# Scattering edge records into cells: indirect DMAs written out one by one, with index and payload read where they lie

## The reference

```
deg = segment_sum(ones, dst)
h = relu(layernorm(x)); x = x + layernorm(h @ Wself.T + (segment_sum(h[src], dst) / deg) @ Wneigh.T + b)
h = relu(layernorm(x)); x = x + normalize(gcn(relu(gcn(h, W1, w)), W2, w))       # edge weight w
h = relu(layernorm(x)); x = x + batchnorm(gru(segment_sum(mlp([h[src], edge_attr]), dst), h))
h = relu(layernorm(x)); x = x + segment_sum(h[src] * w1, dst) @ W3.T + b3        # edge weight w1
```

## Time and profile before

| what | value |
| --- | --- |
| timed runs, median of 3 | 1393.64 us (1392.36 to 1397.23) |
| span of the profiled execution | 1375.1 us |
| median above the span | 18.5 us |
| PE busy | 1233.3 us (90%) |
| DVE busy | 1016.7 us (74%) |
| POOL busy | 704.1 us (51%) |
| ACT busy | 579.8 us (42%) |

### The profile page before, as it was taken

One profiled execution on the slowest core, in us unless ns is written; L12 is line 12 of the kernel. 1 busy time (PEld: TensorE's weight loads), 2 busy tenths in 40 slices (PEclk: granted clock), 3 DMA queues, 4 the chain that ended last, 5 costly groups with the idle time before them and its releaser, 6 DMA issues.

```text
span 1375.1 us, 20029 instructions
## 1 busy us (share of the span) xinstructions
PE 1233.3 (90%) x4504; PEld 751.2 (55%) x4504; DVE 1016.7 (74%) x1944; ACT 579.8 (42%) x1470; POOL 704.1 (51%) x827
## 2 busy tenths in 40 slices
PE   4867989338989889999999989999999899998998
PEld 2533444113333334456876745555555588886787
DVE  9698355138989989853358689999999899888543
ACT  0211221036666660122001168888888833334211
POOL 0577777767877771676677456666666200000000
PEclk9998999769999999999999999999999999999999
DMA  8851521130000006434222677777777300002231
GB/s 331 314 193 64 179 74 63 55 112 18 25 17 19 17 8 267 134 113 144 88 82 90 220 227 230 239 235 236 238 228 242 78 0 1 0 1 88 77 96 37
DMA packets 87257, 167.93 MB, mean 122 GB/s; under 512 B 16124, under 2 KB 44670, under 8 KB 84644
## 3 DMA queue, kind: packets, MB, share of 16 engines
q1 hardware_dynamic: 59588, 102.72, 22.2%
q0 software_dynamic: 25472, 59.97, 14.0%
q10 hardware_dynamic: 2144, 4.59, 1.2%
HBM read 115.97 MB, written 51.25 MB: 122 GB/s over the span
## 4 chain that ended last, share of the span: by engine, by line
PE 56%; issue 14%; POOL 10%; DVE 10%; DMA 5%; DVEq 2%; POOLq 1%; ACT 1%; SPq 0%; ACTq 0%
PE pb L1324 10%; POOL cell_rows L707 9%; PE pb L1224 6%; PE pb L1216 6%; PE pb L1419 5%; PE pb L1392 4%; PE pb L1393 4%; PE pb L1394 4%; PE pb L1338 3%; DVE arena L1675 3%; DMA cell_rows<-tiles,gidx 2%; PE pb L1340 2%; PE pb L1341 2%; PE pb L1190 2%; PE pb L1108 2%
## 5 line engine op out<-in xcount | busy, mean ns | idle before, releaser
L753 POOL DMA_INDIRECT dst_rows<-ering,gidx x168 | 169.4, 1008 | 103.1 <-issue 73.9
L707 POOL DMA_INDIRECT cell_rows<-tiles,gidx x168 | 169.3, 1008 | 68.0 <-issue 40.3
L1324 PE MATMUL pb<-arena 128*128 128x512 f32 x368 | 190.8, 602 | 2.3 <-ACT arena L975 2.3
L1675 DVE TENSOR_TENSOR arena<-pb,arena 128x384 f32 x272 | 151.8, 558 | 25.7 <-PE pb L1190 23.4
L1190 PE MATMUL pb<-arena 128*128 128x384 f32 x272 | 104.9, 512 | 43.8 <-POOL arena L760 43.8
L861 ACT ACTIVATE arena<-iota,free 128x128 f32<-128x128 f32 x272 | 94.3, 393 | 110.2 <-PE pb L1190 68.8
L806 POOL DMA_INDIRECT arena<-p_rows,arena x96 | 98.9, 1030 | 68.8 <-issue 26.7
L1816 DVE TENSOR_TENSOR arena<-pb,arena 128x512 f32<-128x512 f32 x184 | 122.0, 682 | 7.6 <-DMA arena<-p_rows,arena 5.3
L1190 PE MATMUL pb<-tiles,arena 128*128 128x384 f32 x272 | 102.4, 504 | 20.1 <-DVE arena L1675 18.3
L806 POOL DMA_INDIRECT arena<-p_rows,ws x88 | 91.4, 1038 | 44.5 <-issue 24.1
L1340 PE MATMUL pb<-high,low 128*128 128x512 f32 x138 | 108.0, 783 | 2.2 <-DVE arena L1831 1.7
(11 more groups left out here) (306 smaller groups left out, 2583.3 us busy)
## 6 DMA issues: line engine op xcount, KB each, us to landing
dst_rows<-arena SPq DMA_DIRECT2D x6, 2046.0 KB, 17.5
ering<-in_edge_attr_dram SPq DMA_DIRECT2D x41, 256.0 KB, 3.0
arena<-adj SPq DMA_DIRECT2D x10, 640.0 KB, 4.0
arena<-dst_rows SPq DMA_DIRECT2D x24, 264.0 KB, 4.2
arena<-wt_gru SPq DMA_DIRECT2D x48, 128.0 KB, 3.9
ws<-dst_rows SPq DMA_DIRECT2D x22, 264.0 KB, 4.2
arena<-in_x_dram SPq DMA_DIRECT2D x18, 256.0 KB, 9.3
arena<-in_L_gnn_W_hh_dram SPq DMA_DIRECT2D x3, 1024.0 KB, 20.0
```

What stands on the lines that cost most here:

```text
L707: nc.gpsimd.indirect_dma_start(cell_rows[:, :], bass.IndirectOffsetOnAxis(gidx[:, SPAN * a + k:SPAN * a + k + 1], 0), cring[:, a, k], None ...
L753: nc.gpsimd.indirect_dma_start(dst_rows[:, :], bass.IndirectOffsetOnAxis(gidx[:, k:k + 1], 0), ering[:, k, :], None).then_inc(e_scattered[ ...
L1324: nc.tensor.matmul(e_bank(k)[:], erowT[:, k % 4], w1e_sb, start=True, stop=True).then_inc(edge_mm, 1)
L1675: vtt(cell, pb[k % 4][:, 0:3 * P].rearrange("p (m d) -> p m d", m=3), cell, ALU.add).then_inc(block_added, 1)
```

## The change

The indirect DMA of column j now takes its index column straight from `idx1[:, j]` and its payload straight from `pay1[:, j]`. The copies, the payload ring, the semaphore `cells_indexed` and the loops are gone; the 168 DMAs stand in the program one after the other. All DMAs of the even spans raise `c_scattered[0]`, those of the odd spans `c_scattered[1]`, and a span waits at its start until all earlier spans of its parity have landed, so until the span before last has. SP waits for these two semaphores.

```diff
-        gidx = sb("gidx", [P, 2 * SPAN], I32)
-        cring = tiles[:, 3, 0:2 * SPAN * 4].rearrange("p (a c w) -> p a c w", a=2, c=SPAN)
+        gidx = sb("gidx", [P, COL], I32)
...
-        c_scattered = [[sem(f"c_scattered{a}_{k}") for k in range(SPAN)] for a in range(2)]
-        cells_indexed, edges_indexed = sem("cells_indexed"), sem("edges_indexed")
+        c_scattered = [sem(f"c_scattered{a}") for a in range(2)]
+        edges_indexed = sem("edges_indexed")
...
-            for a in range(2):
-                for k in range(SPAN):
-                    full = a == 0 or k < J - SPAN * (SPANS - 1)
-                    sp.wait_ge(c_scattered[a][k], 16 * (SPANS // 2 - (not full)))
+            sp.wait_ge(c_scattered[0], 16 * SPAN * (SPANS // 2))
+            sp.wait_ge(c_scattered[1], 16 * (J - SPAN * (SPANS // 2)))
...
-            def index_span(i, a, n=SPAN):
-
-                for k in range(n):
-                    at_least(pool, c_scattered[a][k], 16 * i)
-                passed()
-                c = bass.ds(SPAN * (2 * i + a), n)
-                nc.gpsimd.tensor_copy(cring[:, a, 0:n], pay1[:, c, :])
-                nc.gpsimd.tensor_copy(gidx[:, SPAN * a:SPAN * a + n], idx1[:, c]).then_inc(cells_indexed, 1)
-
-            def scatter_span(i, a, prepare_next, n=SPAN):
-
-                pool.wait_ge(cells_indexed, 2 * i + a + 1)
-                passed()
-                for k in range(n):
-                    nc.gpsimd.indirect_dma_start(cell_rows[:, :], bass.IndirectOffsetOnAxis(gidx[:, SPAN * a + k:SPAN * a + k + 1], 0),
-                                                 cring[:, a, k], None).then_inc(c_scattered[a][k], 16)
-                if prepare_next:
-                    prepare_next()
-
-            rest = J - SPAN * (SPANS - 1)
+            def scatter_span(span):
+
+                at_least(pool, c_scattered[span % 2], 16 * SPAN * (span // 2))
+                for j in range(SPAN * span, min(SPAN * span + SPAN, J)):
+                    nc.gpsimd.indirect_dma_start(cell_rows[:, :], bass.IndirectOffsetOnAxis(idx1[:, j:j + 1], 0),
+                                                 pay1[:, j], None).then_inc(c_scattered[span % 2], 16)
+
             for n in range(len(BATCHES) - 1):
-                first, last = BATCHES[n] // 2, BATCHES[n + 1] // 2 - 1
-                final = n == len(BATCHES) - 2
                 pool.wait_ge(order_ready[0], n + 1)
                 passed()
-                index_span(first, 0)
-                if last > first:
-                    with pool.Fori(first, last) as i:
-                        scatter_span(i, 0, lambda: index_span(i, 1))
-                        scatter_span(i, 1, lambda: index_span(i + 1, 0))
-                scatter_span(last, 0, lambda: index_span(last, 1, rest if final else SPAN))
-                scatter_span(last, 1, None, rest if final else SPAN)
-
+                for span in range(BATCHES[n], BATCHES[n + 1]):
+                    scatter_span(span)
```

## The result

The changed kernel took 1518.76 us (1517.38 to 1529.47, 4 runs) beside 1395.43 us for the kernel before (1392.36 to 1397.98, 4 runs): a ratio of 1.0909, 95% interval 1.0876 to 1.0942. It is **slower by 123 us**, where 26.5 us less were forecast.

The account below looks back on a forecast made before the run. POOL's own pace in the scatter was taken as the bound, about 33 us behind the next engine. Terms 27.1 + 0.6 - 0.8 - 0.8 = 26.1, or 26.9 from the whole stretch; 26.5 taken: 1393.64 - 26.5 = 1367.1 us, range 1363.5 to 1373.5.

Parts of the forecast that it names:

- Copies, their wait, the loops: POOL's scatter: at 33 boundaries between spans the step falls from 1.12 to 0.30 us, a gain of 27.1 us.
- The first DMA: Start of POOL's scatter: the first indirect DMA starts at about 42.4 instead of 42.99, 0.6 us won.
- The second batch: POOL's eleventh scatter DMA waits for DVE's second batch of indices and starts at 56.1: 0.8 us lost.
- Landings: Scatter: slow landings of a span's last DMA delay POOL at the span after next, 0.8 us lost in all.
- rival B: Scatter: the wait for landings binds in earnest, leaving gains of 8 to 22 us, 1372 to 1386 us; chance 0.09.
- DVE stays ahead from there on: Scatter: DVE's third index batch is complete at 68.3, 13 us after the second, while POOL needs 25 us for the second.
- so nothing new binds: End of the scatter: the table's load lands at 268.6 and DVE is ready at 262.17, 6.4 us before.
- It shifts as a whole: Behind the scatter: all that follows hangs on the table's load by semaphores, so the profiled span falls by 26.5 us.
- With the 18.5 us around it: Whole kernel: 18.5 us lie around the profiled span, so a span of 1348.6 us means a time of 1367.1 us.
- Rival A: The scatter's gain comes as worked out, 22 to 29 us, giving 1365 to 1372 us; chance 0.82.
- Rival C: Scatter: fetching written-out code stalls POOL, 8.0 us a stall; gain 10 to 19 us, or slower at four; chance 0.04.
- Rival D: Behind the table's load, something not tied to it takes 23 us or more; chance 0.03 of same, 0.02 of loss.

Follow-up runs that it names:

- x4_unrolled: The kernel before with only its loops written out, its copies, rings and ten semaphores kept: 1.0008 of the kernel before on chip 14.
- y2_half: The changed kernel with a memset of 430 columns on POOL ahead of each span: 0.9877 of the kernel before on chip 8.
- x1 to x3: The changed kernel with, in turn, a lone instruction after each wait, ten landing semaphores, a tiny memset between spans: 1.0882, 1.0862, 1.0867 of the kernel before, chip 14.
- x3: The changed kernel with a tiny memset on POOL between spans, which nobody waits for: 1.0867 of the kernel before on chip 14.
- y4: The changed kernel with a memset of 230 columns on POOL ahead of each indirect DMA: 1.0011 of the kernel before on chip 8.

## Why the prediction was wrong, point by point

The run on chip 8 (span 1344.2 us) shows the prediction's steps without PE's delay. The profile of before shown in front, span 1375.1, belongs with chips 8 and 4 by its marks: no "remote" wait, ranks done at 98.4 us, and a span like those there (1372 to 1382 us), although the times beside it, 1392 to 1397 us, are like those on 14 and 2. Which chip either pair ran on is not in its records.

Views of the run on chip 8: POOL's timeline, the chain (start, us, what), and the row of windows behind the load:

```profile
42.76 1.19 POOL L694 DMA_INDIRECT cell_rows<-pay,idx  x1 [39.48 <-DVE idx L1505]
...
55.72 0.97 POOL L694 DMA_INDIRECT cell_rows<-pay,idx  x1 [0.30 <-issue]
```

```profile
260.32 2.10 DMA cell_rows<-pay,idx
...
262.49 3.23 DMA free<-cell_rows
...
268.50 6.61 PE pb L1166 x14
```

```profile
262.00:280.00 18.00, 11.50 (x30) 6.47 (x30) 11.49 (x34) 11.00 (x31) 11.59 (x13) 0.72 0.60 213
```

- **Copies, their wait, the loops: right, 27.1 us.** The step is 0.30 at every boundary. From the first DMA's start to the last's it is 260.32 - 42.76 = 217.6 us, before 289.35 - 42.99 = 246.4: 28.8 us less, 27.1 of the copies and 1.7 less busy time in the DMAs (167.6 against 169.3). So **index and payload in place** cost nothing.
- **The first DMA: mis-sized.** The indices were done at 41.67 + 0.17 = 41.84 and the DMA started 0.92 us later, as the gather's did; but they were 0.35 us later than in the trace of before, so 0.2 us were won, not 0.6.
- **The second batch: mis-sized.** No wait at 55.72, where 0.8 us were to be lost: the indices came at 53.3 + 0.18 us instead of 55.2.
- **Landings: mis-sized, 0 in place of 0.8 us**, and rival B falls: neither here nor in the measured run do POOL's waits name a landing. The last DMA landed in 2.10 us. The Trainium skill (DMA: Bandwidth & Descriptors, section on the anatomy of one DMA on the GpSimd path) gives the fixed cost of a DMA as about 2.0 us; the trace agrees.
- **The load** starts at 262.49 (forecast 265), 29.2 us earlier than before. DVE waits 2.8 us for it (forecast 6.4; it was ready at 263.0), PE idles 14.0 us (17), and the rest of the program takes 1344.2 - 262.5 = 1081.7 us (1083.4). PE's clock in 262 to 280 us is 0.72, not 0.50, since PE starts within the stretch. The gain of 30.9 us in span is 4.4 above the sum. The ratio 0.9808 is 26.5 us of 1379.2, but its interval goes from 20 to 33 us, so that it meets the sum to the tenth is luck.
- **"DVE stays ahead from there on" and "so nothing new binds": the steps that failed**, on chips 14 and 2 and in the measurement itself. I took the pace of the engines that feed POOL from the trace of before, and it isn't theirs alone: DVE's batches hang on PE's ranks, and these came late while POOL's DMAs went on without a pause: after one wait of 26.0 us DVE's third batch, due at 68.3, came at 95.2, and later there was one span's ranks in 19.6 us. **"It shifts as a whole"** failed as well: the load of the table was no longer held by POOL's last landing but by PE's products ahead of it in SP's queue. The margin that I counted, 33 us of DVE and 44 us of PE, was the margin of an undisturbed PE. PE's products for the last store ended at 411.50 in place of 253.68, 158 us late, which used it up.
- **"With the 18.5 us around it": a misreading.** The time of each execution in these runs is 1.7 to 1.9 us above its own span. The 18.5 us were mostly the difference between two kinds of chip. The stretch behind the load shows it for the kernel before: 1395.5 - 291.2 = 1104.3 us on chip 14 (x4_unrolled), 1375.1 - 291.7 = 1083.4 in the profile in front; the changed kernel has 1516.6 - 413.8 = 1102.8. The 20 us lie where POOL issues the indirect DMAs of the gather. In the first 500 us behind the load PE is busy for 461.2 us in both kinds; in the next 300 us it executes 900 products in x4_unrolled and 948 in the profile of before (951 on chip 8, 907 in the measured run):

```profile
791.20:1091.20 300.00, 283.08 (x900) 146.10 (x899) 258.59 (x405) 235.13 (x711) 187.31 (x181) 0.99 0.72 220
791.70:1091.70 300.00, 291.74 (x948) 155.14 (x947) 272.79 (x426) 253.99 (x743) 190.27 (x184) 0.99 0.74 224
```

No "remote" wait is named in that stage, and no run tests what slows PE there. That the profile shown and the median shown differed by 1.3% was the one sign, in what I had, that the trace might not be of the machine that would be measured.
- **Rival A** is what the changed kernel shows on chip 8 and nowhere else. **Rival C** falls by x4_unrolled; the instruction queues fetched 27 and 25 pieces in the measured run, before 27 and 26, and none in the 60 us shown above. **Rival D** came nearest: a loss by something that the sum leaves out. But it looked behind the load, and the mechanism lay ahead of it. Its chance of a loss, 0.02, was too small for a stretch whose feeding engines had only been read in one undisturbed trace.

**Shown**: on chips 14 and 2 the loss comes from PE's late semaphores and starts during POOL's chains; on chip 14 the fused wait, the number of semaphores and the lack of a short instruction between spans are not its cause, nor is written-out code; on chip 8 neither the changed kernel nor any of its variants has the delay, and on chip 4 neither of the two variants run there. **Argued only**: that the unbroken pace is what the changed kernel adds. The phases begin 12 to 30 us into each chain and end near its end, and x4_unrolled, the kernel before with its loops written out, has them weakly on chip 14; but index and payload in place are as new as the pace, and no run separates the two on such a chip. **Open**: what in the chip holds PE's signals back, whether its recorder has a part in it (every timed execution was recorded, so none shows the kernel without it), and whether a longer pause prevents it. The versions with the pause of y2_half took 1.0 to 1.4% less than the kernel before on chips 8 and 4 and are untried on 14 and 2; a kernel that must run on all of them can't be chosen from these runs, and the kernel before is the only one known to lose nowhere.

## What to carry to other kernels

Before counting on an engine's slack, ask what feeds the engine that is being made faster, and whether that supply was measured under the new load; POOL's gain of 27 us was real and was worth minus 123 us where its suppliers fell behind. Put the changed kernel itself into every group of experiments as a control, and compare what the kernel before takes there: without it four good runs on another chip read like a cure. A span should fit the times beside it (in all runs here it is 1.7 to 1.9 us below its own time); where it doesn't, the profile is one of other circumstances.

## What was not expected of the hardware

- In the measured run, on chip 2 and on chip 14 (variants x1 to x3), a chain of indirect DMAs on POOL with gaps of 0.30 us (one in 1.27 us) goes with PE's instructions starting in steps of 0.70 us or multiples of it, and with its semaphores being seen late, in the measured run by 4.0 us at first and 16.6 us in the end. DVE's signals to PE arrive within 0.1 us at the same time, and the DMA share is 0.03.
- Chip 8 ran the changed kernel and three variants without any of it, chip 4 two of the variants. On both the kernel before is 1.2% faster than on 14 and 2 (1379 to 1381 against 1397 to 1398 us).
- On POOL a memset of 1, 230 and 430 columns between two indirect DMAs takes 0.12, 0.30 and 0.48 us (x3, y4, y2) and the next DMA starts 0.17 us behind it, or 0.30 behind the DMA before if that is later; waiting for the memset's own semaphore makes it 0.79 us.
